# Attention scores cut into 32x32 and 32x64 tiles of TensorE, and a mask table for each form

## The reference

```python
# attention 0 (self, causal, cut at a length)
energy = einsum('bhsk,bhtk->bhst', Q, K)
energy = where(cols >= lengths, -inf, energy)
energy = where(cols[None, :] > cols[:, None], -inf, energy)
score  = softmax(energy / sqrt(dk))                # dk = 16
# attention 1: the same without the causal line, keys from the context
# attention 2: scores = where(mask_SxS2 == 0, -1e9, scores), a 128x128 mask
# attention 3: scores = where(mask_B == 0, -1e9, scores), a row per batch
# attention 4: 16 heads of 64;  attention 5: 16 heads of 16, both without a mask
```

## Time and profile before

| | us |
|---|---|
| median of 3 runs | 2317.47 (2317.43 to 2318.96) |
| the profiled execution | 2318.61 |
| its span | 2316.8 |
| TensorE matmul busy | 2298.6 |
| TensorE weight load busy | 1980.0 |
| VectorE / ScalarE / GpSimd busy | 1513.0 / 1386.6 / 956.7 |

### The profile page before, as it was taken

The page is one execution under the profiler, slowest core; times in us unless marked ns, Lnnn a source line. Parts: engine busy times, 40 slices in busy tenths (PEclk is TensorE's granted clock), DMA queues, the critical chain, the costliest instruction groups (busy, mean ns, idle before and its releaser), DMA issues.

```text
span 2316.8 us, 74091 instructions
## 1 busy us (share of the span) xinstructions
PE 2298.6 (99%) x30353; PEld 1980.0 (85%) x30353; DVE 1513.0 (65%) x3091; ACT 1386.6 (60%) x3238; POOL 956.7 (41%) x1764
## 2 busy tenths in 40 slices
PE   8999999999999999999999999999999999999998
PEld 7888898888888888888888888888888888888887
DVE  7977654456897665445789776445478977544456
ACT  5566665455567666555656766555465666655555
POOL 3574322233457432223345743223334674322233
PEclk9999999999999999999999999999999999999999
DMA  4400000000100000000010000000001000000000
GB/s 159 143 3 3 2 2 1 1 1 18 37 7 3 3 2 2 1 1 1 25 32 5 3 3 2 2 1 1 1 28 31 4 3 3 2 2 1 1 1 20
DMA packets 23793, 32.51 MB, mean 14 GB/s; under 512 B 2304, under 2 KB 22176, under 8 KB 23328
## 3 DMA queue, kind: packets, MB, share of 16 engines
q1 hardware_dynamic: 23456, 27.78, 3.7%
HBM read 23.57 MB, written 4.19 MB: 12 GB/s over the span
## 4 chain that ended last, share of the span: by engine, by line
PE 98%; issue 0%; DVE 0%; ACT 0%; DMA 0%; POOL 0%; SPq 0%; POOLq 0%; ACTq 0%; DVEq 0%
PE M L583 55%; PE SC L779 16%; PE M L589 12%; PE M L813 7%; PE SC L795 3%; PE M L830 3%; PE SC L627 2%; ACT Pr L985 0%; DMA W<-w_k 0%; DVE nmax L1219 0%; DMA X<-x 0%; PE M L721 0%; POOL Kx L1340 0%; ACT Qx L955 0%; POOL rstd L1388 0%
## 5 line engine op out<-in xcount | busy, mean ns | idle before, releaser
L583 PE MATMUL M<-XT,W 128*128 128x128 f32 x4096 | 511.8, 276 | 0.9 <-DMA W<-w_k 0.9
L583 PEld LDWEIGHTS M<-XT,W 128*128 128x128 f32 x4096 | 496.9, 193 | 17.3 <-issue 11.5
L1219 DVE TENSOR_REDUCE nmax<-SC 128x8 f32<-128x1024 f32 x320 | 390.8, 1221 | 157.1 <-PE SC L779 154.5
L1388 POOL TENSOR_SCALAR rstd<-mv 128x1 f32<-128x1 f32 x256 | 111.8, 437 | 665.5 <-DVE mv L1291 665.5
L985 ACT ACTIVATE Pr<-SC 128x1024 f32<-128x1024 f32 x256 | 262.1, 1024 | 190.6 <-PE SC L779 189.3
L779 PE MATMUL SC<-Qx,Kx 32*128 32x128 f32 x5120 | 372.0, 283 | 0.3 <-issue 0.3
L779 PE MATMUL SC<-Kx,Qx 32*128 32x128 f32 x5120 | 364.5, 280 | 2.1 <-issue 0.4
L779 PEld LDWEIGHTS SC<-Kx,Qx 32*128 32x128 f32 x5120 | 315.9, 186 | 58.8 <-issue 56.3
L779 PEld LDWEIGHTS SC<-Qx,Kx 32*128 32x128 f32 x5120 | 310.7, 186 | 2.5 <-issue 0.9
L1340 POOL TENSOR_SCALAR Kx<-K,own,k_ones 128x128 f32<-128x128 f32 x640 | 286.5, 460 | 23.6 <-PE SC L779 19.8
L955 ACT ACTIVATE Qx<-M,q_bias,q_scale 128x128 f32<-128x128 f32 x640 | 240.9, 457 | 69.7 <-PE M L583 68.1
(11 more groups left out here) (145 smaller groups left out, 4089.7 us busy)
## 6 DMA issues: line engine op xcount, KB each, us to landing
X<-x SPq DMA_DIRECT2D x32, 128.0 KB, 2.3
c_in<-ctx_in SPq DMA_DIRECT2D x32, 128.0 KB, 2.1
out<-X SPq DMA_DIRECT2D x32, 128.0 KB, 1.8
RV<-row_vec SPq DMA_DIRECT2D x1, 2304.0 KB, 8.9
W<-w_k SPq DMA_DIRECT2D x5, 256.0 KB, 3.8
W<-w_q SPq DMA_DIRECT2D x5, 256.0 KB, 4.3
W<-w_v SPq DMA_DIRECT2D x5, 256.0 KB, 4.2
W<-w_f SPq DMA_DIRECT2D x1, 1024.0 KB, 7.1
```

Source lines behind the costliest of these rows:

```text
L583: last = pe.matmul(dst, a, b, start=(k == 0), stop=(k == len(lhsTs) - 1))
L1219: dve.tensor_reduce(nm, SC[h][:, :].rearrange("p (g c t) -> p g c t", c=KC, t=P), AX_X, ALU.max, negate=True).then_inc(maxima, 1)
```

## The change

Each score product is cut along its weight columns, so along the 128 rows of its result: into four products of 32x32 weights where the step holds a unit of attention 0 or 2 (S or T), into two of 32x64 elsewhere. The moving columns are as before, so each piece moves all 128 of them. Both mask tables now hold all four 32-row blocks in both forms, and a mask block uses the row group and the bank of its unit. The tables are twice as large; to make room `c_in` and `q0` are single buffers, and the load of a context stands later in SyncE's order.

```diff
-        put("SP", slot(b, 0) - 2.0, "context", b)
+        put("SP", slot(b, 0) - 0.75, "context", b)
...
-        causal_t, mask_ss_t = sb("causal_t", [P, 4, P], BF16), sb("mask_ss_t", [P, 4, P], BF16)
+        causal_t, mask_ss_t = sb("causal_t", [P, 2, 4, P], BF16), sb("mask_ss_t", [P, 2, 4, P], BF16)
...
-        c_in, CmT = ring(2, "c_in", [P, D]), ring(2, "CmT", [P, D])
+        c_in, CmT = ring(1, "c_in", [P, D]), ring(2, "CmT", [P, D])
...
-        q0 = ring(2, "q0_", [P, 2, P])
+        q0 = ring(1, "q0_", [P, 2, P])
...
-                    if b >= 2:
-                        sp.wait_ge(tile_full, done("tile", ("CT", b - 2)))
+                    if b >= 1:
+                        sp.wait_ge(tile_full, done("tile", ("CT", b - 1)))
...
-                for u, first in ((s_u, 0), (t_u, 2)):
+                for form, u in enumerate((s_u, t_u)):
                     if mask_table(u) is not None:
-                        parts += [(mask_table(u), SC[u % 2], e, first + e) for e in range(2)]
+                        parts += [(mask_table(u)[:, form], SC[u % 2], e, 2 * (u % 2) + e) for e in range(2)]
...
+                for which in (1, 0):
+                    mask = whole(which)
+                    for form in range(2):
+                        bank = SC[1 - which][:, form * 512:(form + 1) * 512]
+                        for j in range(4):
+                            rows = [mask[:, 32 * j:32 * j + 32], ident_b[:, :]] if form else [ident_b[:, 32 * j:32 * j + 32], mask]
+                            for i in range(4):
+                                last = pe.matmul(bank[32 * i:32 * i + 32, j * P:(j + 1) * P], rows[0], rows[1],
+                                                 start=True, stop=True, skip_group_check=True)
+                    last.then_inc(causal_turned, 1)
...
-                    once(tables_done, 1)
+                    once(tables_done, 1 if s_u == 0 else 2)
...
+                    cols = 64 if mask_table(s_u) is None and mask_table(t_u) is None else 32
...
-                                filled[at] = pe.matmul(dst, lhsT, rhs, start=(starting and i == 0),
-                                                       stop=(i == len(line) - 1), skip_group_check=True)
+                                for c in range(0, P, cols):
+                                    filled[at] = pe.matmul(dst[c:c + cols], lhsT[:, c:c + cols], rhs,
+                                                           start=(starting and i == 0), stop=(i == len(line) - 1),
+                                                           skip_group_check=True)
...
-                act.wait_ge(causal_turned, 1)
-                for i, table in enumerate((mask_ss_t, causal_t)):
-                    last = act.activation(chunks(table[:, :, :].rearrange("p j n -> p (j n)")),
-                                          chunks(SC[0][:, i * 512:(i + 1) * 512]), ACT.Copy)
-                last.then_inc(tables_done, 1)
+                for i, table in enumerate((causal_t, mask_ss_t)):
+                    act.wait_ge(causal_turned, i + 1)
+                    act.activation(table[:, :, :, :].rearrange("p f j n -> p (f j n)"), SC[i][:, :],
+                                   ACT.Copy).then_inc(tables_done, 1)
...
-                    if i >= 2:
-                        pool.wait_ge(tile_full, done("tile", ("L", INDEX["q0"][i - 2])))
+                    if i >= 1:
+                        pool.wait_ge(tile_full, done("tile", ("L", INDEX["q0"][i - 1])))
```

More of the change, by code:

```diff
@@ L424, in build @@
         x_loaded, stored = [sem(f"x_loaded{i}") for i in range(LANES)], [sem(f"stored{i}") for i in range(LANES)]
-        c_loaded, m_loaded = [sem(f"c_loaded{i}") for i in range(2)], sem("m_loaded")
+        c_loaded, m_loaded = sem("c_loaded"), sem("m_loaded")
         ready_act, ready_dve, scales_done = sem("ready_act"), sem("ready_dve"), sem("scales_done")
@@ L510, in load_context @@
             def load_context(b):
-                sp.dma_start(c_in[b % 2][:, :], ctx_in[b, :, :]).then_inc(c_loaded[b % 2], 16)
+                sp.dma_start(c_in[0][:, :], ctx_in[b, :, :]).then_inc(c_loaded, 16)
             sp.dma_start(Pr[0][:, 0:C_COLS], consts[:, :]).then_inc(consts_in, 16)
@@ L693, in _ @@
                     b = it[1]
-                    pe.wait_ge(c_loaded[b % 2], 16 * (b // 2 + 1))
-                    turn(tile_of(it), c_in[b % 2], KC).then_inc(tile_full, 1)
+                    pe.wait_ge(c_loaded, 16 * (b + 1))
+                    turn(tile_of(it), c_in[0], KC).then_inc(tile_full, 1)
                 elif kind == "BT":
@@ L1040, in _ @@
                 dve.memset(nmax[i][:, :], 0.0)
-                dve.memset(q0[i][:, :, :], 0.0)
+            dve.memset(q0[0][:, :, :], 0.0)
             dve.wait_ge(consts_in, 16)
```

## The result

The changed kernel takes 2551.61 us (median of 4 runs, 2542.17 to 2553.66), the kernel before, run beside it, 2318.00. The ratio is 1.0999 with an interval of 1.0972 to 1.1027. It is 10% slower; 2300 was predicted. The profiled execution took 2550.8, its span is 2549.0.

The account below looks back on a forecast made before the run. TensorE, busy 99% of the span, was taken to bound the kernel. Whole masks -10, steps without them -8 and start +0.5 made -17.5 us, by the median 2300; range 2270 to 2336.

Parts of the forecast that it names:

- What bounds the kernel, counts, buffers: Whole kernel: TensorE's time stands nearly whole; 50,433 matmuls, some 398 packets; start +0.5 us, `c_in` and `q0` 0.
- The three losses around a masked step: Masks and scores of 152 steps: 0.24 us of 1.47 or 1.44 would go, -36 us if the array kept pace.
- The change of shape: Between masks and scores: switching tile shape costs 0.09 us beyond the 0.11, and goes with one shape, 32x32.
- the masks' stagger: Before a masked step's scores: the wait until the last mask has started, 0.05 us, would go.
- The exposed first weights: Start of a masked step's scores: 128 columns of weights not loaded ahead, 0.10 us, would go.
- The sequencer, 4.4 ns: Masked steps: each instruction takes 4.4 ns to pass, so 288 instructions leave a whole-mask gain of -10 us.
- the lead of 36 instructions: At a masked step's first mask: 36 instructions already passed and waiting, so 252 of 288 remain to be passed.
- The packets: Instruction supply, 256 instructions each, 1.1 us for one; a masked step uses up more than one in 1.2 us.
- The 32x64 steps, -0.045: 183 steps without a whole mask: shorter entry saves 0.07 us, later starts cost some 0.025; -0.045 each, -8 us.
- short supply: Rival, scores of the 152 masked steps: instructions come too slowly and the kernel is slower, 2340 or 2400; chance 0.24.
- the form of 2400: Short supply's worse case: queue holds second records of no more than nine products; 0.6 us more a step, +90.
- a mean price above 4.9 ns: Short supply's threshold per instruction in masked steps, beyond which the loss passes the other steps' 8 us; 5.5 gives 2340.

Follow-up runs that it names:

- uncut: The changed kernel with its scores uncut, 32x128 in all steps; 2317.52 us, ratio 0.9997 to the kernel before.
- every_other: The changed kernel with 32x32 pieces only in masked steps of odd units, 32x128 in all other steps; 2398.64 us, ratio 1.0351 to the kernel before.
- half_moving: `every_other` with each 32x32 piece cut again along its moving columns, into two of 64; 2818.47 us, ratio 1.2146 to the kernel before.

## Why the prediction was wrong, step by step

- *What bounds the kernel, counts, buffers*: right. TensorE's time stood in the result whole, and `uncut` shows tables, `c_in` and `q0` at nothing (+0.5 was forecast).
- *The three losses around a masked step*: right in place. The change of shape and the masks' stagger went, the first score came 0.14 us earlier, 0.23 behind the first mask. The exposed first weights can't be told there from the new price; the 32x64 steps show 0.05 of them gone.
- *The sequencer, 4.4 ns*: this step failed. The price came from runs of 28 and 64 instructions and was laid on 288. It holds about as far as it was seen, and no further. In the changed kernel, behind the 20 stops of over 0.5 us that have enough scores after them, the first 32 records, 64 instructions, start in 0.25 us, 3.9 ns an instruction; the next five records take 0.21, and from there it is 6.6 on average. So 252 x 4.4 = 1.11 should have been 252 x 6.6 = 1.66, and the lead of 36 instructions wasn't there by the time of the first score either: 256 instructions took 1.68 behind it. With 0.23 ahead and 0.20 to the next shape that is 2.11, +0.64 where -0.06 was forecast: +95 us in place of -10.
- *The packets*: the prediction named the place (a masked step uses up more than a packet in 1.2 us) and one packet's time, 1.1 us, but put the wait for one at nothing in its sum. That 1.1 us is the transfer alone. Start to start they are 3.2 us or more apart, so the supply is 12.6 ns an instruction at best. It makes the other half of the loss: 95 us in masked steps, with the clock, and most of the 37 outside them. The Trainium skill (Runtime: NRT & Kernel Launch, Instruction fetch mechanics) says that an engine fetches the next block of 256 instructions while it executes the current one, and that the fetch is hidden, since dispatch is slower than the fill. The blocks of 256 agree with the trace; in this kernel the fill is slower than TensorE's dispatch, 12.6 against 6.6 ns.
- *The 32x64 steps, -0.045*: the entry gained 0.05 as said, but "at 4.6 ns they take 0.59 us of 1.10" failed by the same price: 0.84, no longer below the array's 0.9 with room to spare. +0.033 came of it, +5 us where -8 was forecast; where the cut makes 64 instructions only, the gain is 0.058, near the 0.07 of the earlier trace rows.
- *The rivals*: short supply was the right one, with 0.24, in the form of 2400 still 150 too low. What the text said would show it did: gaps inside masked steps and stops of about 1 us and more. Its other part, a mean price above 4.9 ns, was right too, but stopped at 5.5. Its range ended at 2336 because the price was varied by 1 ns around two short runs; the nearest row for a long run was the densest stretch, 160 instructions in 2.5 us, 16 ns each, and that end was never laid on the sum: 252 x 15.6 + 0.30 = 4.2 us a step, some +420. The truth lay between: 2.73 us for the mean masked step, stops included.

Open stays why 64 instructions pass at 4 ns and a longer row at 6.6, and what a packet waits for in the 3.2 us between starts, of which at least 2.3 us lie between one's landing and the next one's start.

## What to carry to other kernels

Cutting a product into smaller tiles multiplies instructions (four for each float32 product), and where TensorE is busy all the time these have a price of their own. Count the instructions per microsecond over the whole stage. Hold them against two rates, that of the sequencer and that of its packets, and take both from the longest row at such a density that a trace shows; a price read from a short row says nothing of a long one. In this kernel cutting paid where a group stayed at 64 instructions and the entry was what it lost; it lost where a group's instructions took as long as its matmuls, or longer.

## What the runs showed of the hardware

- TensorE's sequencer passed up to 64 instructions at 3.9 to 4.6 ns each, and rows of 128 to 256 at 6.4 to 6.6, with 64 or 128 columns moved by a matmul and in either order of the row groups.
- Packets of 256 instructions were never fetched closer than 3.2 us start to start behind the first 20 us of the kernel before, the changed kernel, `every_other` and `half_moving`, though one lands in 0.9 to 1.7 us; at the stop shown in `half_moving` the DMA share was 0.00 to 0.02.
- A stop of TensorE of 2.1 us (`half_moving`, 314.35) was followed by 5.6 us at the lower level of its clock, so that its full price was above its length.
- Sixteen bfloat16 products of 32x32 that had been waiting started within 0.050 us, 3.3 ns apart, 1.7 for each instruction: what is already in the queue passes faster than the sequencer fills it.
